# Rows for the expert slots: no copies on GpSimd, one product for the sum of squares

## The reference, cut to what matters

```python
y = y * (z * jax.nn.sigmoid(z))                                        # the gated rows, 256 wide
y = y * jax.lax.rsqrt(jnp.mean(y * y, -1, keepdims=True) + EPS) * rms_w
out = y @ W_out.T
# experts: x is the normed row of a token
weights_BTX, indices_BTX = jax.lax.top_k(probs_BTE, TOP_K)             # two experts, two weights
out_BTD = jnp.einsum('BTED,BTE->BTD', down_BTED, full_weights_BTE)
```

## Time and profile before

| | us |
|---|---|
| median of 3 runs (lowest to highest) | 794.01 (790.43 to 794.33) |
| the profiled execution | 795.79 |
| its span, first to last instruction | 794.0 |
| PE busy, share of the span | 631.2 (79%) |
| DVE busy | 585.2 (74%) |
| ACT busy | 462.3 (58%) |
| POOL busy | 400.4 (50%) |

### The profile page before, as it was taken

One profiled execution on the slowest core, in us unless ns is written; L12 is line 12 of the kernel. 1 busy time (PEld: TensorE's weight loads), 2 busy tenths in 40 slices (PEclk: granted clock), 3 DMA queues, 4 the chain that ended last, 5 costly groups with the idle time before them and its releaser, 6 DMA issues. The chain is left out here.

```text
span 794.0 us, 15139 instructions
## 1 busy us (share of the span) xinstructions
PE 631.2 (79%) x3701; PEld 531.9 (67%) x3703; DVE 585.2 (74%) x1410; ACT 462.3 (58%) x1014; POOL 400.4 (50%) x601
## 2 busy tenths in 40 slices
PE   0695629998999989999998998699898889988700
PEld 0695317777778777778777776587777777777600
DVE  7787898898898888888898888555565555654445
ACT  0352446688777878877788775454555555554400
POOL 3000006576766766766676767145555555555510
PEclk9999999799999999999999999799999999999955
DMA  9950100000000000000000015133333333333169
GB/s 306 266 130 0 29 1 23 19 27 23 29 22 22 28 22 22 28 22 22 25 26 22 29 24 184 36 88 99 97 85 96 88 98 98 85 98 86 54 252 382
DMA packets 64647, 61.43 MB, mean 77 GB/s; under 512 B 9242, under 2 KB 55710, under 8 KB 64624
## 3 DMA queue, kind: packets, MB, share of 16 engines
q1 hardware_dynamic: 56176, 44.11, 19.7%
q0 software_dynamic: 8448, 17.06, 6.2%
HBM read 30.19 MB, written 31.47 MB: 78 GB/s over the span
## 5 line engine op out<-in xcount | busy, mean ns | idle before, releaser
L449 POOL DMA_INDIRECT moe_d<-raw,slot_st x136 | 133.8, 984 | 124.6 <-issue 102.1
L422 POOL DMA_INDIRECT slots_d<-rows,slot_st x128 | 134.6, 1052 | 73.8 <-POOL rows L417 52.5
L1040 DVE SCALAR_TENSOR_TENSOR act<-raw,taps,act 128x512 f32<-128x512 f32 x192 | 149.3, 785 | 23.9 <-ACT act L513 23.1
L398 POOL TENSOR_TENSOR xde<-xb,e_end 128x256 f32<-128x256 f32 x64 | 45.6, 713 | 113.2 <-DVE xb L1117 111.6
L1233 DVE CAST x_hi<-bank 128x256 fp32r<-128x256 f32 x68 | 28.8, 424 | 95.4 <-PE bank L871 91.8
L864 PE MATMUL bank<-xw_hi,x_hi 128*128 x136 | 61.1, 449 | 27.2 <-DVE x_lo L1235 22.7
L774 PE MATMUL bank<-xb,m_sb 128*128 128x64 f32 x512 | 75.9, 298 | 3.8 <-POOL xde L398 3.8
L774 PEld LDWEIGHTS bank<-xb,m_sb 128*128 128x128 f32 x512 | 73.1, 216 | 5.6 <-issue 3.9
L890 PE MATMUL bank<-act,raw 128*128 x544 | 72.0, 275 | 1.8 <-issue 1.8
L664 ACT ACTIVATE raw<-bank 128x256 f32<-128x256 f32 x68 | 26.5, 391 | 77.2 <-remote 68.5
L890 PEld LDWEIGHTS bank<-act,raw 128*128 128x128 f32 x544 | 66.1, 192 | 1.9 <-issue 1.9
(11 more groups left out here) (231 smaller groups left out, 1659.4 us busy)
## 6 DMA issues: line engine op xcount, KB each, us to landing
slots_d<-rows SPq DMA_DIRECT2D x8, 1122.0 KB, 13.4
rows<-slots_d SPq DMA_DIRECT2D x68, 132.0 KB
x_sb<-in_x SPq DMA_DIRECT2D x8, 512.0 KB, 7.0
act<-in_x SPq DMA_DIRECT2D x64, 64.0 KB
xw_hi<-moe_d SPq DMA_DIRECT2D x8, 512.0 KB, 9.3
xw_lo<-moe_d SPq DMA_DIRECT2D x8, 512.0 KB, 9.9
out<-x_sb SPq DMA_DIRECT2D x8, 512.0 KB, 13.5
moe_d<-raw,slot_st POOLq DMA_INDIRECT x136
```

The lines of the kernel that those rows point to most:

```text
L398: nc.gpsimd.tensor_tensor(by_head(xde[:, u, :]), by_head(xdt[:, u, :]), per_head(e_end, nn), ALU.mult).then_inc(xde_done, 1)
L422: nc.gpsimd.indirect_dma_start(out=slots_d, out_offset=bass.IndirectOffsetOnAxis(ap=slot_st[:, r, c:c + 1], axis=0), in_=rows[:, r, c, :], ...
L449: nc.gpsimd.indirect_dma_start(out=moe_d, out_offset=bass.IndirectOffsetOnAxis(ap=slot_st[:, r, c:c + 1], axis=0), in_=ym[r][:, c * D:(c + ...
L1040: V.scalar_tensor_tensor(out=group_act(par)[:, t, :], in0=proj[:, t, k:k + GT], scalar=taps[:, t, k:k + 1], in1=group_act(par)[:, t, :], o ...
```

## The change

POOL makes no copies for the scatter any more. The row for the second choice is written by ACT: L569 now writes both choices in one instruction, with its input broadcast over them (128 x 256 in place of 128 x 128). Token number, weight and slot number come by a DMA of SP, one for each tile, from `meta`, which now has four numbers for each choice (the slot number's bits in the third); the scatters read the slot number from the row itself. SP issues these loads behind the two `dd` loads of each pair of tiles. `slot_i` is gone, and so is `row_done`; `ld_id` takes its place.

POOL gets one new instruction for each tile: it adds the two halves of `sq` (`add_halves`, two tiles behind), and PE multiplies only that sum by the column of ones. PE's `project_out` so waits for POOL (`sq_sum`) in place of ACT (`sq_done`).

```diff
@@ sync, dd_loads @@
                     sp.dma_start(dd_r[8:10, i % 2, :].bitcast(F32), cs_d[:, bass.ds(n * NH * P, 2 * NH * P)])\
                         .then_inc(ld_dd[i % 2], 16)
+                    id_load(b, 2 * i)
+                    id_load(b, 2 * i + 1)
+
+            def id_load(b, j):
+                r = j % R
+                if is_first(b) and j < R:
+                    sp.wait_ge(slots_done, 1)
+                    sp.wait_ge(st_zero, 16 * 8)
+                else:
+                    sp.wait_ge(scat[r], 16 * K * (b * 2 + j // R))
+                sp.dma_start(rows[:, r, :, D:D + 4], meta[:, tile_ix(b * SC + j), :, :]
+                             .rearrange("p a k v -> p (a k) v")).then_inc(ld_id[r], 16)
@@ gpsimd @@
-            def prepare_ids(b, j):
...
-            def prepare_rows(b, j):
-
-                nn, r = b * SC + j, j % R
-                pool.wait_ge(xn_done, nn + 1)
-                pool.sem_inc(scatters, 1)
-                nc.gpsimd.tensor_copy(rows[:, r, 1, 0:D], rows[:, r, 0, 0:D]).then_inc(row_done, 1)
-                pool.wait_ge(row_done, 3 * (nn + 1))
+            def rows_ready(b, j):
+
+                r = j % R
+                pool.wait_ge(xn_done, b * SC + j + 1)
+                pool.wait_ge(ld_id[r], 16 * (b * 2 + j // R + 1))
                 pool.sem_inc(scatters, 1)

             def scatter(r, c):
                 nc.gpsimd.indirect_dma_start(
-                    out=slots_d, out_offset=bass.IndirectOffsetOnAxis(ap=slot_st[:, r, c:c + 1], axis=0),
+                    out=slots_d, out_offset=bass.IndirectOffsetOnAxis(ap=slot_of[:, r, c, :], axis=0),
                     in_=rows[:, r, c, :], in_offset=None).then_inc(scat[r], 16)
+
+            def add_halves(nn, u):
+
+                pool.wait_ge(sq_done, nn + 1)
+                nc.gpsimd.tensor_tensor(sq[:, u, 0:P], sq[:, u, 0:P], sq[:, u, P:2 * P], ALU.add).then_inc(sq_sum, 1)

             def sequence(b):
                 for j in range(SC):
                     nn = b * SC + j
-                    prepare_ids(b, j)
...
-                    prepare_rows(b, j)
+                    rows_ready(b, j)
                     scatter(j % R, 0)
                     scatter(j % R, 1)
                     if not (is_last(b) and j == SC - 1):
                         inputs_to_end(nn + 1, (j + 1) % 2)
+                    if not (is_first(b) and j < 2):
+                        add_halves(nn - 2, j % 2)
@@ scalar, row @@
-                A(rows[:, r, 0, 0:D], x_sb[:, t, :].rearrange("p a d -> p (a d)"), ACT.Identity,
+                A(rows[:, r, :, 0:D], x_sb[:, t, :].broadcast_to([P, K, D]), ACT.Identity,
                   bias=nmr1[:, t], scale=r1[:, t]).then_inc(xn_done, 1)
@@ tensor, project_out @@
-                pe.wait_ge(sq_done, nn + 1)
+                pe.wait_ge(sq_sum, nn + 1)
...
-                for c in range(2):
-                    m = mm(bank[7][:, D:D + 1], sq[:, u, c * P:(c + 1) * P], ones[:, 0:1], start=(c == 0),
-                           stop=(c == 1))
-                m.then_inc(o_done, 1)
+                mm(bank[7][:, D:D + 1], sq[:, u, 0:P], ones[:, 0:1], start=True, stop=True).then_inc(o_done, 1)
```

## The result

The changed kernel took 801.32 us (median of 4 runs, 799.83 to 804.98), the kernel before 792.22 us beside it: ratio 1.0121, 95% interval 1.0077 to 1.0166. Forecast were 790.7 us and a range up to 798.0. The profiled execution took 802.11 us with a span of 800.4, against 795.79 and 794.0.

A forecast was written before the change was run, and what follows sets the result against it. PE was taken to lead, with a DVE leg nearly as long at q = 1 and 2 and POOL bounding the last group. Terms -2.8 - 2.5 + 1.0 + 1.0 = -3.3 us gave 790.7 us, range 783.0 to 798.0.

The forecast's parts named there:

- One product in place of two: PE's product of squares with ones: saves 0.19 us a tile, counted only at q = 0 of 15 groups, -2.8 us.
- ACT's longer row: ACT's L569 writing both choices: 0.10 us more a tile, hidden by ACT's waits, so costed at nothing.
- POOL's copies: Copies gone from POOL, addition in: net 0.7 us a tile, counted only in the last group, -2.5 us.
- In the last group it is the path for four tiles: POOL bounds the last group, which has no project work, so its saving counts there for four tiles: 2.8 us.
- 0.3 us back: At the very end the last tiles pass from ACT over POOL to PE, which returns 0.3 us of the gain.
- The new wait: PE's wait for POOL's sum (`sq_sum`): tightest at q = 3, falling in the 0.92 us silu wait; nothing.
- about 0.5 a group, 7 us: Price set on PE's wait for POOL's sum if the silu wait failed to cover it.
- SP's new loads: Small loads on SP's queue, issued some two tiles ahead of use, `dd` loads behind an old wait: nothing.
- The clock: PE's idle stretch around the silu grows 0.2 to 0.4 us; one dip-free group lost, +1.0 us, bounds 0 and 3.8.
- VectorE and GpSimd: Mutual hindrance on the DVE leg as POOL's scatters start earlier: between -0.2 and +0.43 us a group, taken as +1.0.
- Rival C: GpSimd's earlier scatter falls on DVE's gate in each group: slower, +7.6 us, 801.6 us; chance 0.12.
- Rival B: Middle groups gain nothing, the q = 0 saving being met by dips in all groups: -0.5 us, 793.5 us; chance 0.12.

The follow-up runs named there:

- after_twice: Changed kernel with PE's single product of the sum with the ones issued twice, waits unchanged; 769.64 us, 1.0055 of the kernel before.
- rows_wfirst_fill: Changed kernel without addition (two products), experts' first weights issued before the last two entry loads, six useless PE products a group; 774.81 us, 0.9800 of the kernel before.
- before_fill_2: Kernel before with six useless PE products per group in the silu wait; 780.62 us, 0.9854 of the kernel before.
- after_wfirst: Changed kernel with the experts' first weights issued ahead of the last two entry loads on SP; 770.55 us, 1.0080 of the kernel before.
- the repeat: Changed kernel run once more with nothing altered; 803.25 us, 1.0095 of the kernel before.
- halves_only: Kernel before with only POOL's addition and the single product added, copies still on POOL; 789.3 us, 1.0331 of the kernel before.

## Why the prediction was wrong

The steps, in the order in which the prediction has them.

- **One product in place of two, -2.8 us.** Failed. The product's time is gone from PE's work, but PE is not ahead of anything with it: it waits longer around the silu instead, and `after_twice` has the product back and is not slower. With the clock held, 0.83 us less of PE work in a pair of groups goes with 0.86 us more of time.
- **ACT's longer row, nothing.** Right in size (0.611 us), and no cost of it shows: `rows_wfirst_fill` has it and is 0.42 us a pair of groups faster than `before_fill_2`.
- **POOL's copies, -2.5 us in the tail.** POOL's part was right: 0.16 to 0.17 us ahead of the first scatter, a step of 4.25 us where it doesn't wait (xde at 489.29 and 493.54; 4.4 expected), and with the weights first POOL's last scatter comes 3 us sooner after the silu, with the sum (`after_wfirst`, 21.6) or without it (`rows_wfirst_fill`, 21.6). But nothing of it reached the end. "In the last group it is the path for four tiles" was the step that failed: with POOL faster, PE waits for DVE and its work on the experts' weights next, and I had named nothing in its place. Nor does the last scatter hold the experts' first tile, as I had read from the 1.29 us in the earlier trace rows: that wait is 1.29 or 1.30 us in all 14 profiles, in 13 of them it ends with ACT's `tok`, and in before, too, the tile starts 0.86 us after the end of `tok` (504.86), as in the others. The tail ends with PE's last output. The term "0.3 us back" was too small as well: PE waits 1.71, 0.94 and 0.90 us for the sum there. And that the middle groups gain nothing was wrong the other way: the rows are worth 0.2 us a group, some 3 us over 14.
- **The new wait, nothing.** The step that failed most. The argument was that at q = 3 it falls in the silu wait. It does, and the silu does not wait for it. But PE does: four of ten times 1.37 to 1.39 us for the sum at that place. With the clock held the sum, single product included, costs 0.43 us a group on top of the rows, some 6 us over 14 groups, where the forecast had nothing; "about 0.5 a group, 7 us", its price for the case that the argument failed, was right. PE's idle time around a silu grows from 1.63 to 2.08 us; I had counted only the 0.92 of it in the earlier trace rows and left out its wait for `tok` ahead of the silu. The addition was also mis-sized: 0.46 us at most tiles, 0.9 and more at some (0.51 to 0.57 on the mean), for 0.36.
- **SP's new loads, nothing.** Failed in the tail. I named the `dd` loads behind the new waits and not the experts' weights, which stand in the same queue. The tail is 3.1 us longer in this profile, and issuing the weights first takes back 1.2 to 3.3 us in three pairs of profiles.
- **The clock, +1.0 us, bounds 0 and 3.8.** The idle stretch grew about as expected (0.45 us; 0.2 to 0.4 taken). What the clock costs was wrong (0.4 to 0.6% of the time by the medians, 3 to 5 us), and the bounds were drawn wrongly: they allowed one short dip behind each silu, and two groups had long ones, +4.9 us together in the profiled execution, above the 3.8. The evidence stood in the trace of before:

```profile
139.67:166.67 27.00, 25.51 (x134) 21.14 (x134) 23.65 (x54) 18.87 (x40) 17.29 (x30) 0.81 0.07 22
```

  I counted dips and did not look at their lengths.
- **VectorE and GpSimd, +1.0 us.** About nothing: L1047 takes 783 ns on the mean (782 before), the gate 457 (469). Rival C, the scatter on the gate, named nearly the measured time (801.6), but that is luck, since its mechanism is wrong: the steady groups are not longer (23.87 and 23.90 us for 23.85 and 24.22), and the gate is not slower. `xde` is, 778 ns for 714.

Rival B, nothing left in the middle and dips in all groups, came nearest in kind and was still too mild: it had them all of one length, and no cost for the sum. No rival had the sum's wait and the clock together.

What stays open: what makes some dips long, and which executions have them. They are at the same place in the profiles of the result and of the repeat, absent from that of `after_wfirst` with the same recurrence, and in `halves_only` 7 of the 13 groups behind 166 us are over 25.5 us. The size of PE's wait in front of them does not decide it (2.30 + 1.14 us in one profile, 1.47 + 0.43 in the other). Nor is it shown how much of the whole loss is the clock's: the medians say 0.4 to 0.6 of 1.0 to 1.2%, the profiles of single executions from nothing to that.

## What to carry to other kernels

Work that is moved from the engine that leads to one behind it adds a handover. Here the time saved on the leading engine turned into waiting, and the handover cost more than the saving even at a full clock. Price it as idle time of TensorE, and look at what the profile's granted clock does behind such waits; do not put it down as a wait that another one hides. When a load moves to a queue, list everything that stands behind its wait up to the next stage. And before saving TensorE work, try filling its short waits: here six useless products a group gave 1.5%, where the change was forecast to give 0.4%.

## What was not expected of the hardware

- The granted clock falls to its lower level (0.5 of full, 1.2 GHz) behind most silus around which PE idles 1.4 to 2.3 us in two pieces (11 of 15 before, one of them behind a single piece of 2.65 us; three of the four without stand behind 1.44 to 1.50 us); L783 then takes 1.80 us for 1.00. Products of no use in that wait keep it at 1.00 from 160 to 450 us in all five kernels that have them, and bring a group of the kernel before from 23.79 to 22.84 us on the mean.
- The stretches at the lower level are not of one length: most cost 1.7 us (one minus the clock, summed), a few 3.4 or 5.1, behind silus of the same kind, and not in every execution of the same code.
- A 128 x 128 addition of two SBUF operands on GpSimd takes 0.44 to 0.48 us in most tiles and 0.90 to 0.98 in some (8 of 64 in the changed kernel); what they fall together with was not tested. A 128 x 128 copy on GpSimd goes from 375 to 530 ns on the mean when the addition joins it.
